# Rotary halves swapped by DMA instead of by ScalarE, V's bound in a score buffer's column, and half of k's rounding on GpSimd, in a one-core transformer layer

## The reference, cut to what matters

```
q = (x @ Wq + bq) * scale          # per head [1024, 128]
k = x @ Wk + bk
v = x @ Wv + bv
q, k = t * cos(pos) + rotate_half(t) * sin(pos)      # for t = q and t = k
attn = softmax(where(causal, -max, q @ k.T))
x = layernorm(x + (attn @ v) @ Wo + bo)
x = layernorm(x + down(silu(gate(x)) * up(x)))
```

## Time and profile before

| | before |
|---|---|
| median of 3 runs | 1923.18 us (1920.52 to 1923.53) |
| the profiled execution | 1920.36 us |
| its span, first to last instruction | 1918.6 us |
| mean granted TensorE clock | 0.990 |
| TensorE busy | 1778.1 us (93%) |
| ScalarE busy | 1591.1 us (83%) |
| VectorE busy | 1573.9 us (82%) |
| GpSimd busy | 1246.2 us (65%) |

### The profile page before, as it was taken

The page is one execution under the profiler, slowest core; times in us unless marked ns, Lnnn a source line. Parts: engine busy times, 40 slices in busy tenths (PEclk is TensorE's granted clock), DMA queues, the critical chain, the costliest instruction groups (busy, mean ns, idle before and its releaser), DMA issues. The chain is left out here.

```text
span 1918.6 us, 33748 instructions
## 1 busy us (share of the span) xinstructions
PE 1778.1 (93%) x10464; PEld 1406.3 (73%) x10464; DVE 1573.9 (82%) x3748; ACT 1591.1 (83%) x2910; POOL 1246.2 (65%) x1041
## 2 busy tenths in 40 slices
PE   6899999989999999999999999999999999989997
PEld 5677777767777777767777777777777776768886
DVE  6788888888888888888888888888888888876886
ACT  6888888888899888889988899888898988863443
POOL 4667776677666667776767766677766666624554
PEclk8999999999999999999999999999999999989999
DMA  3655565556555656565555655765656775550001
GB/s 97 157 110 111 110 130 114 112 117 134 113 114 116 137 116 110 111 145 116 117 114 104 133 114 114 138 131 115 115 104 110 158 131 100 98 121 12 23 23 34
DMA packets 638257, 210.01 MB, mean 109 GB/s; under 512 B 609408, under 2 KB 622208, under 8 KB 636672
## 3 DMA queue, kind: packets, MB, share of 16 engines
q1 hardware_dynamic: 614400, 165.91, 45.2%
q10 hardware_dynamic: 23680, 41.95, 7.3%
HBM read 48.40 MB, written 8.39 MB: 30 GB/s over the span
## 5 line engine op out<-in xcount | busy, mean ns | idle before, releaser
L848 DVE SCALAR_TENSOR_TENSOR planes<-S,recip,planes 128x128 f16<-128x128 f32 (+7 forms) x512 | 417.3, 815 | 94.0 <-ACT planes L657 91.2
L657 ACT ACTIVATE planes<-S,recip 128x128 f16<-128x128 f32 (+7 forms) x512 | 379.0, 740 | 129.8 <-DVE recip L899 115.9
L423 POOL TENSOR_TENSOR swap<-swap,sin_t 128x512 f32<-128x512 f32 x256 | 331.3, 1294 | 190.4 <-ACT swap L665 190.2
L648 ACT ACTIVATE S<-p_row,neg_max 128x128 f32<-128x128 f32 (+7 forms) x512 | 380.0, 742 | 51.7 <-DVE neg_max L838 44.5
L838 DVE CUSTOM_DVE_ANT_0 p_row<-S,mask_row 128x128 f32<-128x128 f32 (+7 forms) x512 | 385.1, 752 | 27.8 <-PE S L1112 26.3
L417 POOL TENSOR_TENSOR rot<-rot,swap 128x512 f32<-128x512 f32 x252 | 323.0, 1282 | 72.4 <-DVE rot L889 69.8
L665 ACT ACTIVATE swap<-S,bqk 64x512 f32<-64x512 f32 x512 | 349.8, 683 | 18.7 <-DVE wmax L706 5.9
L1112 PE MATMUL S<-QKA 128*128 128x512 f32 (+4 forms) x1152 | 262.7, 355 | 5.0 <-DVE rot L889 4.5
L1112 PE MATMUL S<-QKB 128*128 128x512 f32 (+4 forms) x1152 | 259.6, 352 | 2.6 <-DVE planes L848 2.2
L439 POOL TENSOR_TENSOR QKA<-rot,QKA 128x512 fp32r<-128x512 f32 x124 | 160.1, 1291 | 122.3 <-ACT QKA L491 122.1
L1063 PE MATMUL O<-PT,VB 128*128 128x512 f16 (+3 forms) x1152 | 217.6, 330 | 22.8 <-issue 14.2
(11 more groups left out here) (129 smaller groups left out, 2931.2 us busy)
## 6 DMA issues: line engine op xcount, KB each, us to landing
w_raw<-in_w_heads ACTq DMA_DIRECT2D x64, 256.0 KB, 2.7
wv_raw<-in_w_heads ACTq DMA_DIRECT2D x32, 256.0 KB, 3.5
PT<-planes SPq DMA_TRANSPOSE x512, 3.4
wo_raw<-in_wo_heads ACTq DMA_DIRECT2D x32, 256.0 KB, 3.8
attn_d<-resid ACTq DMA_DIRECT2D x4, 1024.0 KB, 6.7
x_raw<-in_x_cols SPq DMA_DIRECT2D x3, 1024.0 KB, 5.9
resid<-in_x_rows ACTq DMA_DIRECT2D x3, 1024.0 KB, 5.4
resid<-in_x_rows SPq DMA_DIRECT2D x2, 1024.0 KB, 6.7
```

The costliest lines, as they stand in the source:

```text
L423: nc.gpsimd.tensor_tensor(swap[:, c, :], swap[:, c, :], sin_t[:, half], ALU.mult).then_inc(sin_done, 1)
L648: nc.scalar.activation(row_psum(n, s)[:, 0:cols], p_row[:, k % 2, 0:cols], ACT.Exp, bias=neg_max[:, s:s + 1], scale=-1.0, accum_out=row_su ...
L657: nc.scalar.activation(row_halves(n, s)[:, 0], row_psum(n, s)[:, 0:cols].rearrange("p (j q) -> p j q", q=P), ACT.Copy, scale=recip[:, s:s ...
L848: nc.vector.scalar_tensor_tensor(halves_of[:, 1], row_psum(n, s)[:, 0:cols].rearrange("p (j q) -> p j q", q=P), recip[:, s:s + 1], halves_ ...
```

## The change

It does five things.

1. chunk_out writes the chunk with its bias straight into a new SBUF buffer, proj, in one instruction of 128 partitions. SyncE then issues two DMAs for each chunk, each of which copies 64 partitions of proj into the other half of swap. They come in slots 0 to 3, behind that slot's transpose. GpSimd's product with sin waits for their landing.
2. The high part of k (chunks 1 and 3) is copied by GpSimd in slots 4 and 6. ScalarE keeps the high part of q.
3. The four one-column matmuls write into column 511 of the score buffer of row 1, just ahead of that row's scores in slot 1 of the even step, and no longer into X. Their wait for `added` is gone. The two waits on `scaled` in output and values go too; values has one on `v_lo` instead.
4. VectorE reads the bound (take_bound) in slot 1 ahead of the row's mask, and makes the two factors in slot 1 after the row's reciprocal.
5. weigh moves from slot 3 of the even step to slot 5 of the odd step ahead of it.

```diff
+    def bound_psum(pair):
+        return X[:, GQ - 1:] if pair == 0 else row_psum(2 * pair - 2, 1)[:, GQ - 1:GQ]
...
@@ sync
+                    if project and s < 4:
+                        swap_halves(n + 1, s)
...
+            def swap_halves(m, c):
+                sp.wait_ge(chunk_sb, n_four(m, c))
+                wait(sp, rot_done, n_four(m - 1, c))
+                for lo, hi in ((0, D // 2), (D // 2, 0)):
+                    sp.dma_start(swap[lo:lo + D // 2, c, :], proj[hi:hi + D // 2, c, :]).then_inc(swapped[c], 16)
@@ gpsimd
-                        pool.wait_ge(chunk_sb, 2 * n_four(m, c))
+                        pool.wait_ge(swapped[c], 32 * (m + 1))
...
+                    if project and s in (4, 6):
+                        c = s - 3
+                        pool.wait_ge(rot_done, n_four(m, c))
+                        half = slice((c // 2) * GQ, (c // 2 + 1) * GQ)
+                        nc.gpsimd.tensor_copy(QK[1 - par][:, 1, 0, half], rot[:, c, :]).then_inc(k_hi, 1)
@@ scalar
-                    if project and 3 <= s < 7:
+                    if project and s in (3, 5):
...
-                wait(act, rot_done, n_four(m - 1, c))
-                for lo, hi in ((0, D // 2), (D // 2, 0)):
-                    nc.scalar.activation(swap[lo:lo + D // 2, c, :], row_psum(n, c)[hi:hi + D // 2, GQ:], ACT.Identity,
-                                         bias=bqk[hi:hi + D // 2, c % 2, m % H:m % H + 1]).then_inc(chunk_sb, 1)
+                wait(act, swapped[c], 32 * m)
+                nc.scalar.activation(proj[:, c, :], row_psum(n, c)[:, GQ:], ACT.Identity,
+                                     bias=bqk[:, c % 2, m % H:m % H + 1]).then_inc(chunk_sb, 1)
@@ vector
+                        if makes_v(n) and par == 0 and s == 1:
+                            take_bound((n >> 1) + 1)
                         masked_scores(n, s)
...
-                    if own and makes_v(n) and par == 0 and s == 6:
+                    if own and makes_v(n) and par == 0 and s == 1:
                         scale_up((n >> 1) + 1)
...
-                    if own and makes_v(n) and par == 0 and s == 3:
-                        weigh((n >> 1) + 1)
+                    if par == 1 and s == 5 and makes_v(n + 1):
+                        weigh((n + 3) >> 1)
@@ tensor
-                if pair == 1:
-                    pe.wait_ge(v_lo, n_v_all(0))
-                elif pair > 1:
-                    pe.wait_ge(added, n_added(2 * pair - 2, 0))
...
+                    if makes_v(n) and par == 0 and s == 1:
+                        bound_of((n >> 1) + 1)
...
-                    if own and makes_v(n) and par == 0 and s == 6:
-                        bound_of((n >> 1) + 1)
```

More of the change, by code:

```diff
@@ L85, in layer @@
     rot = sb("rot", [P, 4, GQ])
+    proj = sb("proj", [P, 4, GQ])
     ident = sb("ident", [P, P])
@@ L120, in layer @@
     X = pb("X", GQ)
-    bound_psum, fold_psum = X[:, GQ - 1:], X[:, 0:DIM]
+    fold_psum = X[:, 0:DIM]
     def row_psum(n, s):
         return S[(8 * n + s) % 3]
+    def bound_psum(pair):
+        return X[:, GQ - 1:] if pair == 0 else row_psum(2 * pair - 2, 1)[:, GQ - 1:GQ]
     def folds(n):
@@ L146, in layer @@
         sem(n) for n in ("scored", "attended", "chunked", "v_made", "wo_made"))
-    exped, high, chunk_sb, rot_hi, v_hi, o_hi = (
-        sem(n) for n in ("exped", "high", "chunk_sb", "rot_hi", "v_hi", "o_hi"))
+    exped, high, chunk_sb, q_hi, k_hi, v_hi, o_hi = (
+        sem(n) for n in ("exped", "high", "chunk_sb", "q_hi", "k_hi", "v_hi", "o_hi"))
     maxed, low, cos_done, rot_done, v_lo, recip_ok, added = (
@@ L155, in layer @@
     sin_done, rot_lo, o_lo = (sem(n) for n in ("sin_done", "rot_lo", "o_lo"))
+    swapped = [sem(f"swapped{c}") for c in range(4)]
     def n_scored(n, s):
@@ L433, in run @@
                                                 halves(xT, 0, half).bitcast(F32), ALU.subtract).then_inc(x_lo, 1)
+                    if project and s in (4, 6):
[3 more added lines that the diff above has]
+                        nc.gpsimd.tensor_copy(QK[1 - par][:, 1, 0, half], rot[:, c, :]).then_inc(k_hi, 1)
                     if project and 3 <= s < 7 and n >= 0:
                         c = s - 3
-                        pool.wait_ge(rot_hi, n_four(m, c))
+                        pool.wait_ge((q_hi, k_hi)[c % 2], 2 * m + (c // 2 + 1))
                         half = slice((c // 2) * GQ, (c // 2 + 1) * GQ)
@@ L572, in run @@
                         act.wait_ge(rot_done, n_four(m, c))
-                        copy(QK[nxt][:, c % 2, 0, half], rot[:, c, :]).then_inc(rot_hi, 1)
+                        copy(QK[nxt][:, 0, 0, half], rot[:, c, :]).then_inc(q_hi, 1)
                     if n < 0 and s in (3, 4):
@@ L712, in weigh, with take_bound @@
                                         ).then_inc(weighed, 1)
+            def take_bound(pair):
+                dve.wait_ge(bounded, pair + 1)
+                wait(dve, scaled, 3 * pair)
+                nc.vector.tensor_scalar(bound[:, :], bound_psum(pair), 1e-30, 1.0 / UP, ALU.max, ALU.mult
+                                        ).then_inc(scaled, 1)
             def scale_up(pair):
                 at = slice(pair % 2, pair % 2 + 1)
-                dve.wait_ge(bounded, pair + 1)
-                nc.vector.tensor_scalar(bound[:, :], bound_psum, 1e-30, 1.0 / UP, ALU.max, ALU.mult
-                                        ).then_inc(scaled, 1)
                 dve.wait_ge(scaled, 3 * pair + 1)
                 nc.vector.reciprocal(v_up[:, at], bound[:, :]).then_inc(scaled, 1)
-                dve.wait_ge(scaled, 3 * pair + 2)
-                nc.vector.tensor_scalar(pv_down[:, pair % 3:pair % 3 + 1], bound[:, :], 1.0 / UP, None, ALU.mult).then_inc(scaled, 1)
+                nc.vector.tensor_scalar(pv_down[:, pair % 3:pair % 3 + 1], bound[:, :], 1.0 / UP, None, ALU.mult
+                                        ).then_inc(scaled, 1)
             dve.wait_ge(bias_in, 16)
@@ L788, in run @@
                     if n < 0 and s == 4:
+                        take_bound(0)
                         scale_up(0)
@@ L815, in run @@
                         half = slice((c // 2) * GQ, (c // 2 + 1) * GQ)
-                        dve.wait_ge(rot_hi, n_four(m, c))
+                        dve.wait_ge((q_hi, k_hi)[c % 2], 2 * m + (c // 2 + 1))
                         sub(QK[nxt][:, c % 2, 1, half], rot[:, c, :], QK[nxt][:, c % 2, 0, half].bitcast(F32)
@@ L886, in rotate_cos @@
                 half = slice((c // 2) * GQ, (c // 2 + 1) * GQ)
-                dve.wait_ge(chunk_sb, 2 * n_four(m, c))
+                dve.wait_ge(chunk_sb, n_four(m, c))
                 wait(dve, rot_lo, n_four(m - 1, c))
@@ L1043, in bound_of @@
                 pe.wait_ge(weighed, pair + 1)
-                if pair == 1:
-                    pe.wait_ge(v_lo, n_v_all(0))
-                elif pair > 1:
-                    pe.wait_ge(added, n_added(2 * pair - 2, 0))
                 for t in range(KT):
-                    last = mm(bound_psum, ones[:, :], bprod[:, t:t + 1], start=t == 0, stop=t == KT - 1)
+                    last = mm(bound_psum(pair), ones[:, :], bprod[:, t:t + 1], start=t == 0, stop=t == KT - 1)
                 last.then_inc(bounded, 1)
@@ L1076, in output @@
                         pe.wait_ge(xt_lo, KT)
-                elif i == 1 and makes_v(nn):
-                    pe.wait_ge(scaled, 3 * (nn >> 1) + 4)
                 elif i == 3:
@@ L1141, in values @@
                     elif n == 1 and i == 0:
-                        pe.wait_ge(scaled, 4)
+                        pe.wait_ge(v_lo, n_v_all(0))
                     elif n > 0:
```

## The result

The change gives **1910.13 us** (median of 20 runs, 1904.27 to 1921.22) against 1920.88 for the kernel before beside it (20 runs, 1917.87 to 1926.12). The ratio is 0.9947, with 0.9933 to 0.996 as its 95% interval: 10.7 us faster, where 66 were forecast, and outside the forecast's range. The profiled execution took 1905.75 us, with a span of 1903.9.

The account below looks back on a forecast made before the run. TensorE bounds odd steps, the ScalarE-VectorE row chain even ones. Pair gain 3.12 us less 0.6 (weigh) and 0.3 (GpSimd) leaves 2.2; 31 pairs give 68, less 2 at start: 1854 profiled, 1857 median, range 1823 to 1900.

Parts of the forecast that it names:

- Is that covered?: GpSimd's chain to chunk 1's low part: 0.4 us late in even steps; 0.3 us a pair charged, between 0 and 1.5.
- an even step could take 23.96 + 0.44 = 24.40: Even step at TensorE's pace: the odd step's 23.96 us plus 0.44 for the bound's four one-column matmuls, instead of 27.52.
- 0.7 + 2.7 us: Chunk 0's copies on SyncE's queue: 0.7 us for two issues plus 2.7 to land, from 926.3 to some 930.
- far from full: SyncE's queue: eight copy issues at 0.33 us, 2.6 us a step, beside eight transposes of 1.2 to 1.9 us.
- The slower rival: SyncE's queue: issues from about 1.6 us make transposes late, pair 53 us, 1970 us in all; chance 0.07.
- weigh: VectorE's 1.58 us moves from the even step to the odd; 0.6 us charged to the odd step, between 0 and 1.58.
- The wait ahead of the bound: TensorE's 1.21 us wait in each even step until VectorE has read X, 36.1 us in all, goes.
- The copy of k: GpSimd's copy of k's high part: taken as 1.0 us, with 0.7 to 1.3 us as the sign of being right.
- The first head's scores: Start of the kernel: a DMA landing less the shorter copy costs 2 us once, between 0 and 6.
- GpSimd's chain as the bound of even steps: Rival: copies of k at 1.29 us and landings 1.5 us later cost 1.5 us more a pair, 1895 us; chance 0.12.
- VectorE pays weigh in full: Rival: weigh's 1.58 us is not absorbed in the odd step, gain 1.2 us a pair, 1885 us; chance 0.06.
- The wait for X: TensorE's 1.21 us wait ahead of the bound in even steps, 36.1 us in all, contained in the 3.12 us pair gain.

Follow-up runs that it names:

- the kernel without copies: The change without its 512 DMA copies: GpSimd multiplies the unswapped chunk in proj by sin, so the rotation is left out; 1855.08 us, ratio 0.9653.
- Part 1 alone: The kernel before with only the swap by DMA added; 1937.43 us, ratio 1.0084.
- parts 3 to 5 alone: The kernel before with only the bound's new place, its reading and weigh's move; 1920.34 us, ratio 1.0.
- parts 2 to 5: The change without part 1: ScalarE's two halves swap the chunks again; 1894.38 us, ratio 0.9865.

## Why the prediction was wrong

**The step that failed** is the one under "Is that covered?", the charge of 0.3 us a pair for GpSimd's chain. The steps 1 to 62 of the change are 44.3 us longer than those of the kernel without copies, which is 1.43 us a pair and just inside the 1.5 that I kept as the upper end. The rest of the 49.0 us between the two spans is 5.3 in the start and step 0, less what the end gives back. The forecast held 11.3 us for all this. So 38 of the 52 us by which the profiled execution (1905.75) misses 1854 are here.

The other 14 us come from a second step, "an even step could take 23.96 + 0.44 = 24.40". Measured between first scores, as there, the undisturbed steps without copies are 25.39 and 24.15, a pair of 49.54 where the sum without GpSimd's 0.3 said 48.96. The earlier trace rows had shown TensorE busy for 24.96 us in the even step, more than the 24.40 that I gave it.

What was wrong in the first:

- *One landing, where there are two.* I let ten instructions follow chunk 0's landing at the pitch of 1.26 us. That landing was right: 4.5 us later than before in the even step (8.16 against 3.62 us into the step), as forecast. But chunk 1's copies have a landing too, and it comes last. Without a wait for it chunk 1's product would start at 11.9 in an even step, 0.5 us before the edge, and at 11.0 in an odd one. It starts at 12.49 and 11.60 at the median, and as late as 17.2.
- *A value, where there is a spread.* I took 0.7 + 2.7 us as if they were fixed. The trace gives 2.2 us from an issue to its landing at the least, 3.0 at the median and 7.3 at the most. A chain that ends at the edge pays every late landing in full and gets nothing for an early one; here 29.1 us in 27 steps.
- *Seven steps with transfers of 1 MB* beside the copies carry 16.1 of these 29.1 us (steps 8, 24 and 40 have the load of x on the same queue, ahead of chunk 1's copies, 27.3 to 28.7 us against 25.1 to 25.4 without copies). I had not looked for them.
- *SyncE "far from full".* I had averaged over the step. In slots 0 to 3 the queue has no gap, and an issue takes 0.59 us at the median, not the 0.33 of ScalarE's row. In the step shown, four pairs of issues (6.0 us) and three transposes (3.7) fill 975.27 to 985.57. The slower rival wanted 1.6 us an issue, which the median did not reach. Part 1 alone is slower than before all the same; its largest wait is GpSimd's 524 us for landings.
- *weigh.* I charged the odd step 0.6 us, the same in every step, and saw no link to the copies. Its second instruction takes 0.16 to 1.23 us by what GpSimd does just then, and late copies move that.

**What held, and what did not.** ScalarE's busy time, 1340 against 1336 forecast. The wait ahead of the bound is gone. GpSimd's first product with sin starts 4.5 us later in the even step. Not held: of the forecast steps of 24.5 to 25.0 and 24.0 to 24.8 us the medians, 25.78 and 25.09, miss both. In the kernel without copies the odd step keeps its 24.40 (24.38 before) although it now has weigh, and ScalarE's relief may be what pays for it; with parts 3 to 5 alone the odd steps paid 0.6. The product of two columns takes 560 ns at the median instead of 904. The copy of k takes 0.62 us, the lower end of my range, and not 1.0:

```profile
L453 POOL CAST QKA<-rot 128x512 fp32r<-128x512 f32 x64 | 39.6, 619 | 2.5 <-DVE rot L830 2.5
```

By the tight-loop figure of the Trainium skill (GPSIMD Engine Reference, performance versus the Vector engine) it would have been, as an estimate, 0.77; the trace decides for 0.62. The first head's scores were late by 3.4 us instead of 2.

**The rivals.** GpSimd's chain as the bound of even steps was the right mechanism, and I gave it 0.12. Its own list of conditions (copies of k at 1.29 us, landings 1.5 us later) was not what brought it about. I had even reckoned the even step's chain 0.4 us past the edge, and still charged almost nothing. "VectorE pays weigh in full", at 0.06, named the other mechanism, the product of two columns that waits for GpSimd's instruction; its price was too high, its place right.

**Of the credit.** The 27 us that parts 2 to 5 give alone, and 39 more from halving ScalarE's swap work if nothing were paid for it (1894.4 to 1855.1), make the 66. The wait for X, 36 us in the waits, gave nothing with weigh moved alone. Less of ScalarE's work gave more: chunk 3 by DMA saves 64 instructions of 683 ns, 44 us of work, and gave 25 us; it took the even step from 25.91 to 25.15, where the kernel without copies stands too.

## What to carry to other kernels

Where a transfer is put into a chain, compute the latest start that costs nothing for each of its landings, not only for the first. If the median lands within a microsecond of that edge, charge the spread: here, with the median on the edge, 27 of 62 steps lost 29 us, more than half of it in seven steps with large transfers. Then move only those transfers that have room: two of four chunks by DMA gave 1866 us, against 1910 for all four and 1894 for none.

Ask of an issuing queue whether it has a gap in the slots in question, not over the step. A wait's length is no proof of its value: TensorE's wait was removed, with weigh moved, in a stage that another engine bounds, and nothing was gained. And before a product of two operands in SBUF, like weigh's second, is put into a tight stage of VectorE, look at what GpSimd does there.

## What I had not expected of the hardware

- VectorE's product of two columns (two inputs in SBUF) took 0.16 us with GpSimd at rest and, in the change, up to 1.23 us beside it. In the change and in the kernel before it ended 0.02 us behind GpSimd's running instruction each time that it took 0.3 us or more.
- An issue of a copy on ScalarE's queue took 0.53 us at the median and kept ScalarE from its next instruction; two of them per chunk made the kernel 144 us slower than the same copies on SyncE's queue (2053.8 against 1910.1).
- Landings of like copies, issued at the same place of like steps, differed by 1.2 us in the two steps shown and by up to 1.6 among the even steps without large transfers (issues ended at 8.7 in both, chunk 1's product at 12.07 in one and at 13.63 in the other).
- 67 MB of copies that nobody waits for, beside the ring's other 166 MB, cost 14 us in 1855 and left the undisturbed even steps at 25.15.
- Chunk 1's copies landed 3.50 us behind the end of their issue at the median in even steps, beside a load of 256 KB on ScalarE's queue, and 1.85 and 1.81 us in the two steps without it.
